# Scan stage: the B blocks of even pairs are copied out of their PSUM bank by ScalarE, and VectorE adds their three later taps from the copy

## What is computed

```python
zxbcdt = u @ in_proj_w.T
xBC = zxbcdt[..., D_INNER:D_INNER + CONV_DIM]
xBC = causal_conv1d(xBC, conv_w, conv_b)          # 4 taps along the tokens, each channel by itself
Bm = xBC[..., D_INNER:D_INNER + N_HEADS * D_STATE].reshape(b, l, N_HEADS, D_STATE)
Cm = xBC[..., D_INNER + N_HEADS * D_STATE:].reshape(b, l, N_HEADS, D_STATE)
...
seg = jnp.exp(cum[:, :, :, None, :] - cum[:, :, None, :, :])
cb = jnp.einsum('bcihn,bcjhn->bcijh', Cr, Br)
scores = jnp.where(mask[None, None, :, :, None], seg * cb, 0.0)
y_intra = jnp.einsum('bcijh,bcjhp->bcihp', scores, xr)
```

## Time and profile before

| | |
|---|---|
| median of 3 runs | 1132.34 us (1130.03 to 1136.43) |
| the profiled execution | 1130.17 us |
| its span in the profile | 1128.4 us |
| mean granted PE clock | 0.971 |
| busy share of the span | PE 89%, DVE 70%, ACT 48%, POOL 34% |
| the scan of round 1 (277.88 to 372.00 us) | PE 88.39, DVE 82.02, ACT 76.63, POOL 55.47 us busy of 94.12 |

### The profile page before, as it was taken

One profiled execution on the slowest core, in us unless ns is written; L12 is line 12 of the kernel. 1 busy time (PEld: TensorE's weight loads), 2 busy tenths in 40 slices (PEclk: granted clock), 3 DMA queues, 4 the chain that ended last, 5 costly groups with the idle time before them and its releaser, 6 DMA issues.

```text
span 1128.4 us, 21206 instructions
## 1 busy us (share of the span) xinstructions
PE 1005.3 (89%) x7808; PEld 614.2 (54%) x7808; DVE 789.1 (70%) x1763; ACT 544.6 (48%) x1154; POOL 388.2 (34%) x601
## 2 busy tenths in 40 slices
PE   6899797899998998989998998988998998979666
PEld 3445545654454666654454666654555666647442
DVE  4888635678889655678888646678888536675435
ACT  3888521346887321446887221446887211431312
POOL 3567201132666011142665011132674101131652
PEclk9999999899999999999999999999999999988978
DMA  6899300003444000003433000004445504005557
GB/s 213 312 297 297 109 1 19 1 2 99 148 133 130 1 1 19 20 2 123 139 133 117 1 1 19 20 2 132 134 140 169 142 1 112 20 1 150 161 213 297
DMA packets 74743, 113.64 MB, mean 101 GB/s; under 512 B 6167, under 2 KB 64670, under 8 KB 73744
## 3 DMA queue, kind: packets, MB, share of 16 engines
q1 hardware_dynamic: 71952, 104.48, 29.0%
q0 software_dynamic: 1536, 3.60, 1.0%
q10 hardware_dynamic: 1152, 4.19, 0.9%
HBM read 93.46 MB, written 19.40 MB: 100 GB/s over the span
## 4 chain that ended last, share of the span: by engine, by line
PE 53%; DVE 21%; ACT 11%; issue 8%; POOL 5%; DMA 1%; SPq 0%; DVEq 0%; POOLq 0%; ACTq 0%
PE bank L957 19%; DVE hf L1825 8%; PE bank L1033 5%; DVE turned_p L2085 4%; PE bank L1238 3%; PE bank L1280 3%; ACT hf L1487 2%; PE bank L1324 2%; PE bank L1327 2%; PE bank L970 2%; ACT dec L1542 2%; POOL rs L1651 2%; PE bank L1379 1%; PE bank L948 1%; ACT nmax L1504 1%
## 5 line engine op out<-in xcount | busy, mean ns | idle before, releaser
L957 PE MATMUL bank<-uT,w_in 128*128 128x512 f32 (+1 forms) x584 | 272.1, 607 | 15.7 <-DVE hf L1825 13.0
L1825 DVE SCALAR_TENSOR_TENSOR hf<-bank,conv_w,hf 128x510 f32<-128x510 f32 (+2 forms) x232 | 169.5, 744 | 35.9 <-ACT yg L1496 27.7
L957 PEld LDWEIGHTS bank<-uT,w_in 128*128 128x128 f32 (+1 forms) x584 | 102.5, 188 | 133.9 <-issue 87.4
L1651 POOL TENSOR_TENSOR rs<-ve,half 128x2 f32<-128x2 f32 x56 | 38.9, 695 | 294.5 <-DVE ve L1969 294.5
L1487 ACT ACTIVATE hf<-bank,conv_b,conv_w 128x512 f32<-128x512 f32 x128 | 98.7, 771 | 62.4 <-PE bank L957 62.4
L1124 PE MATMUL bank<-hf 64*64 64x128 f32 (+3 forms) x2048 | 89.9, 307 | 13.9 <-issue 8.0
L1124 PEld LDWEIGHTS bank<-hf 64*64 64x64 f32 x2048 | 75.1, 135 | 44.4 <-issue 29.9
L957 PE MATMUL bank<-uT,w_gu 128*128 128x512 f32 x224 | 99.0, 593 | 0.0
L1465 ACT ACTIVATE xc<-bank 128x512 f32<-128x512 f32 x44 | 26.3, 597 | 114.0 <-PE bank L957 77.1
L2266 DVE TENSOR_REDUCE nmax<-bank 128x2 f32<-128x256 f32 (+1 forms) x128 | 65.4, 553 | 20.3 <-PE bank L1327 18.1
L1714 POOL TENSOR_TENSOR hf<-hf,yg 128x506 f32<-128x506 f32 x52 | 65.9, 1267 | 25.3 <-DVE hf L1839 21.4
(11 more groups left out here) (343 smaller groups left out, 2121.1 us busy)
## 6 DMA issues: line engine op xcount, KB each, us to landing
hf<-cum_dram SPq DMA_DIRECT2D x32, 384.0 KB, 3.6
dec<-cum_dram SPq DMA_DIRECT2D x32, 384.0 KB, 3.6
tmp<-cum_dram SPq DMA_DIRECT2D x32, 384.0 KB, 3.6
x<-cum_dram SPq DMA_DIRECT2D x32, 384.0 KB, 3.5
y_dram<-xf SPq DMA_DIRECT2D x16, 512.0 KB, 6.0
w_in<-in_w_in SPq DMA_DIRECT2D x1, 3584.0 KB, 11.4
w_in<-in_w_egu SPq DMA_DIRECT2D x6, 512.0 KB, 9.3
w_in<-y_dram ACTq DMA_DIRECT2D x5, 512.0 KB, 10.6
```

The costliest lines, as they stand in the source:

```text
L957: mm = pe.matmul(plan[key][0:n, :], w[:, k, cols], uT[:, k, :], start=k == 0, stop=k == DC - 1)
L1651: pool.tensor_tensor(rs[:, cols], ve[:, cols], half[:, cols], ALU.pow).then_inc(rstd_ready.sem, 1)
L1825: ins = dve.scalar_tensor_tensor(d, x, conv_w[:, j, TAPS - 1 - s:TAPS - s], d, ALU.mult, ALU.add)
```

## The change

For the even pairs 2 to 14 (`raw_pairs`) ACT copies the whole B block from bank 0 into the SBUF tile `nmax` (`copy_raw`, 128x512 fp32) right behind the first tap, and this copy frees bank 0. DVE adds the same three taps as before, but reads `nmax` in place of the bank (`taps_from_raw`). `nmax` is also the place of the product of the odd pairs' B blocks, so the two uses take turns: the copy of pair p waits for POOL's addition of pair p - 1 (`b_conv_sum`), and the product of pair p for DVE's taps of pair p - 1 (`raw_taps`). PE's products for an even pair wait for `raw_taps` too, since the freed bank no longer says that the taps are done.

```diff
+        raw_pairs = list(range(2, PAIRS - 1, 2))
+        raw_b = nmax[:, :, :, :].rearrange("p a i q -> p (a i q)")
...
+                            if w == 0 and p in raw_pairs:
+                                pe.wait_ge(raw_taps.sem, raw_taps.at(r, raw_pairs.index(p) + 1))
...
                 def b_tap_product(p):
 
                     key, n = ("BC", p, 0), shared_taps.index(p)
+                    act.wait_ge(raw_taps.sem, raw_taps.at(r, raw_pairs.index(p - 1) + 1))
+                    x = plan[key][:, :].rearrange("p (b l) -> p b l", b=SEQS)[:, :, 0:SEQ - TAPS + 1]
+                    act.activation(first_product, x, ACT.Copy, scale=conv_w[:, 2 + p, 0:1]).then_inc(b_tap3.sem, 1)
+
+                def copy_raw(p):
+
+                    key, n = ("BC", p, 0), raw_pairs.index(p)
                     if n > 0:
                         act.wait_ge(b_conv_sum.sem, b_conv_sum.at(r, n))
-                    x = plan[key][:, :].rearrange("p (b l) -> p b l", b=SEQS)[:, :, 0:SEQ - TAPS + 1]
-                    act.activation(first_product, x, ACT.Copy, scale=conv_w[:, 2 + p, 0:1]).then_inc(b_tap3.sem, 1)
+                    act.activation(raw_b, plan[key][:, :], ACT.Copy).then_inc(plan.drains(key), 1)
...
+                        if b == 0 and p + 2 in raw_pairs:
+                            copy_raw(p + 2)
...
+            def taps_from_raw(r, p):
+
+                dst, j = bc[:, p % 3, 0, :], 2 + p
+                raw = raw_b.rearrange("p (b l) -> p b l", b=SEQS)
+                dve.wait_ge(*plan.drained(("BC", p, 0), r))
+                for s in range(1, TAPS):
+                    d = dst.rearrange("p (b l) -> p b l", b=SEQS)[:, :, s:SEQ]
+                    ins = dve.scalar_tensor_tensor(d, raw[:, :, 0:SEQ - s], conv_w[:, j, TAPS - 1 - s:TAPS - s], d,
+                                                   ALU.mult, ALU.add)
+                    if s < TAPS - 1:
+                        link(ins)
+                    else:
+                        ins.then_inc(raw_taps.sem, 1)
...
+                    if w == 0 and p in raw_pairs:
+                        taps_done[0] += 1
+                        taps_from_raw(r, p)
+                        return
```

More of the change, by code:

```diff
@@ L418, in sandwich @@
         b_conv_sum = signal("b_conv_sum", len(shared_taps))
+        raw_taps = signal("raw_taps", len(raw_pairs))
         decayed = signal("decayed", 64)
```

## The result

The changed kernel takes 1143.21 us (median of 4 runs, 1140.55 to 1143.8) beside 1132.47 us (1130.03 to 1136.43) of the kernel before in the same comparison: a ratio of 1.0094, interval 1.0074 to 1.0114. It is slower by 10.7 us; 1146 was predicted, with 1141.5 to 1151 as the range. Its profiled execution took 1143.64 us, with a span of 1141.9. The repeat at the end of the experiments gave a median of 1142.53 us, and its single executions lie between 1136.66 and 1145.62.

What follows compares the result with a forecast made beforehand. PE, 89% busy, was taken as the bound, with the scan's period set through bank 1. Rounds 1 to 3 at 3.8 us each plus round 0's 2.3 made 13.6 us, giving 1146 us, likeliest 1141.5 to 1151, 8-in-10 range 1137 to 1157.

Steps and rivals of the forecast that it cites:

- Step (1): ACT's 28 copies, about 595 ns each, delay the exponentials and C's product queued behind by 0.50 us per even pair.
- the loop through bank 1: PE projects, ACT makes C's product, DVE adds C's taps, PE projects again: all in sequence, closing in 11.63 us.
- Step (2): Bank 0 free at 318.96, not 320.80: nothing in the period, 0.3 us gained at pair 3, 0.43 absorbed at pair 13.
- e: Lengthening of a two-pair period: 0.50, 0.54 or 0.88 us by masks between; taken as 0.75, in round 0 as 0.50.
- Step (3): DVE's three taps cost 2.31 us from SBUF as from the bank; C's taps keep 0.30 us of slack.
- Step (4): POOL's masks take turns with DVE's taps from SBUF, 0.34 us each; C's taps kept 0.04 us by one, 0.38 by both.
- a sign that POOL's part is misread: Sign in the profile after: a two-pair period over 12.6 us, where 12.1 to 12.5 was expected in rounds 1 to 3.
- Step (5): New waits of the copy on POOL's addition and the odd product on the taps have 2 to 5 us slack, costing nothing.
- round 0's, 6 x 0.50 - 0.73 = 2.3 us: Round 0's scan loses 2.3 us: its masks wait longer for the DMA and mostly come after the taps.

Runs made afterwards that it cites:

- experiment 5: Changed kernel with the second head's two exponentials of the next even step moved behind C's first tap and product on ACT: 1138.75 us, ratio 1.0058.

## Why the prediction was right, and where its sizes were off

Step (1), the copy costs 0.50 us in the loop through bank 1: shown. The copy put by itself into the kernel before costs 0.52 us a period; in the changed kernel ACT's next instruction starts 0.48 us later, and PE's stalls are at L1852. There the copies took 586 ns; 595 were taken.

Step (2), bank 0 free early gives nothing in the period and 0.3 us at pair 3: right in kind. With the delay but without the release a scan takes 92.5 us, with both and no masks in the way 92.0. The release is worth 0.5 us a scan, of which some 0.2 lies at pair 3 (from pair 2 to 4 the changed kernel takes 12.21 to 12.32 us where it is 12.49 without the release; without masks in the way 12.25 to 12.45), 0.15 in the regular periods (12.12 against 12.16 each) and 0.14 between pairs 12 and 14 (12.13 against 12.27). The sum had a cost of e - 0.43 at pair 12, which is 0.32 us with its e of 0.75 and 0.07 with no mask; measured were 0.09 us with one mask between (12.36 against 12.27) and, without masks, a gain of 0.14.

Step (3), the taps cost the same from SBUF, and C's taps have 0.30 us of slack: shown by the masks that only write (2.31 us, and 0.30 us idle).

Step (4), POOL's masks take turns with the taps: shown. The step's values for e were 0.50 with no mask between, 0.54 with one, 0.88 with both. Measured were 0.48 to 0.52 with one (12.12 to 12.16 us), since the slack takes it in, and 0.80 to 0.99 with both (12.44 to 12.63); the upper end is over the 12.6 that the forecast named as a sign that POOL's part is misread, by 0.03. In the period shown first two masks cost the taps 3.02 - 2.31 = 0.71 us, of which the slack took in half. Over the twelve regular periods of rounds 1 to 3 the mean of e is 0.75 us, and 0.71 in the repeat. That the forecast had 0.75 is in part luck, for it was a choice between the values for one mask and for two. The loss was 3.9, 3.5 and 2.8 us a scan in rounds 1 to 3, a mean of 3.4, where the prediction had 3.8. This term was over-sized by 0.4 a round, and not in the regular periods: pair 12 cost 0.10 us where the sum had 0.32, and pair 14, beside whose taps no late_keys mask runs, 0.48 where it had 0.75; against that pair 2 gained 0.2 in place of 0.3.

Step (5), the new waits cost nothing: the changed kernel's waits show none on `raw_taps` that holds an engine on the path; right.

**The term that was wrong is round 0's, 6 x 0.50 - 0.73 = 2.3 us.** The scan took 91.84 us before and 92.27 after: 0.4. The regular periods after are 12.13 us there but for one of 12.42, in which PE's products wait 0.72 us for POOL's addition, so the cost of 0.50 each did come; but the periods before were not the 11.64 and 12.27 of the other rounds. Three of them took 11.99, 12.95 and 12.53 us, together 1.9 us more. The timelines of POOL, and of PE at two places, in the kernel before:

```profile
73.46 0.76 POOL L1693 TENSOR_SCALAR_AFFINE_SELECT tmp<-tmp 128x256 f32<-128x256 f32 x2 [2.20 <-DMA tmp<-cum_dram]
...
75.42 1.42 POOL L1697 TENSOR_TENSOR x<-x,late_keys 128x256 f32<-128x256 f32 x2
76.78 1.26 POOL L1714 TENSOR_TENSOR hf<-hf,yg 128x506 f32<-128x506 f32 x1
```

```profile
53.72 1.32 PE L1124 MATMUL bank<-hf 64*64 64x256 f32 x32 [0.72 <-POOL hf L1714]
...
78.30 1.32 PE L1124 MATMUL bank<-hf 64*64 64x256 f32 x32 [1.68 <-DVE hf L1825]
```

PE's products need the C block with POOL's addition (L1714), and that stands in POOL's queue behind masks and selects which wait for their DMA, at 73.46 for 2.20 us. At 53.72 the profile names it. At 78.30 it ended at 76.78 + 1.26 = 78.04, just ahead of the products; the DVE taps that the row names end at about the same time, but in the other rounds the same products start before the third B tap is done (319.29 against 320.80), so they don't wait for it. With masks that only write, and are short, the kernel before has 11.63 or 11.64 us in all four regular periods of round 0, and only the one from pair 12 to 14 is long, 12.67. The other profiles fit: those with a regular period under 12 us and reading masks have one to three longer ones in round 0, up to 13.09 us, while the kernel with the unused copy and the repeat of the changed one have 12.12 to 12.16 in all of theirs. The prediction had read that round 0's masks wait longer for the DMA and used it only for how often they get between taps. That the same lateness already cost the kernel before 1.9 us, which a longer period then hides, was not looked at.

The sum over the four rounds, from the profiled executions of the two kernels: 0.4 + 3.9 + 3.5 + 2.8 = 10.6 us, against 10.7 of the medians. Predicted were 13.6. Of the 3.0 too many 1.9 are round 0's and 1.1 those of the other three rounds. The mechanism of both parts was right, the copy's delay in the loop through bank 1 and the turns with POOL.

## What to carry to other kernels

Before an instruction is put into an engine's queue to free a buffer sooner, look at what is queued behind it: here ACT's copy freed one bank some 1.8 us sooner (by the forecast's estimate from the rows before) and the other 0.5 us later, and both had been just in time. Of two buffers that both come free just in time, freeing one gave next to nothing; ask which order of the work that is there already serves both, as moving two exponentials did (0.3% faster with nothing added). When an operand moves from PSUM to SBUF, look at what GpSimd reads at that time: two masks between made three taps 0.7 to 0.9 us longer in the changed kernel, one mask 0.3 to 0.4, and how many got between differed from round to round. When a cost is added up over rounds, look whether the kernel before is as fast in each of them: what was already late there hides a part of the cost.

## What was not expected of the hardware

Between the scans of rounds 0 and 1, where the change does nothing, the two profiled executions differ. The windows of this stretch, in the kernel before and in the changed one (us, busy us of PE, PEld, DVE, ACT, POOL, granted clock):

```profile
135.00:212.00 77.00, 63.94 (x220) 40.74 (x220) 33.66 (x127) 16.67 (x35) 7.58 (x10) 0.91 0.03 7
```

```profile
136.00:216.00 80.00, 66.86 (x218) 42.37 (x219) 33.38 (x126) 16.72 (x34) 7.64 (x11) 0.87 0.02 7
```

The same work (no engine's count differs by more than two) takes 3 us longer, at a granted clock of 0.87 over the stretch in place of 0.91. From round 0's scan to round 1's it was 151.25 us in this one profile of the kernel before, 152.2 in the first one with the exponentials moved there, and 154.5 to 156.5 in the ten others. So of the 13.5 us between the two spans some 3 don't come from the change, which the medians, 10.7 us apart, bear out. Two profiles of kernels that differ by one per cent have to be compared stage by stage, with the granted clock beside each.

Not all of POOL's reading costs the taps alike. The timelines of DVE and POOL in round 0 of the changed kernel with masks that only write:

```profile
65.03 2.36 DVE L1861 SCALAR_TENSOR_TENSOR hf<-nmax,conv_w,hf 128x510 f32<-128x510 f32 x3 [0.79 <-ACT nmax L1515]
```

```profile
65.26 1.59 POOL L1706 TENSOR_SCALAR_AFFINE_SELECT hf<-hf 128x256 f32<-128x256 f32 x2 [1.31 <-DMA hf<-cum_dram]
```

Two selects, 0.77 us when free, took 1.59 beside the taps, and the taps 2.36 in place of 2.31: here POOL was kept, and DVE hardly. Two masks in that place cost DVE 0.7 to 0.9 us. But a select can hold a tap too: at 323.60 in experiment 5 the first tap took 1.00 us in place of 0.75 beside two that had begun at 323.29, while the selects here began with a tap already running. What decides it was not tried.
